# Four broadcasts moved from SyncE's DMA queue, slot 40, to ScalarE's own queue, slot 41

## The reference

```python
h = tok(x)                      # 4x4 patches: 256 tokens of 64 per image, 16 pixels attended per token
h = h + mamba(layernorm(h))     # two selective scans (forward, backward), 128 channels, 16 states
h = h + pkm(layernorm(h))       # 8 heads: product keys pick 16 of 4096 table rows; causal attention; output product
```

```python
x_dbl = x @ W_xproj.T
Bm, Cm = x_dbl[..., 16:32], x_dbl[..., 32:48]       # per token, the same for all channels
h_t = exp(delta_t * A) * h_(t-1) + (delta_t * x_t) * Bm_t
y_t = sum over states of h_t * Cm_t
```

## Time and profile before

| | |
|---|---|
| device time, median of 3 (lowest to highest) | 12621.17 us (12620.08 to 12621.36) |
| profiled execution, its own time | 12642.72 us |
| span of its trace, instructions | 12640.9 us, 260041 |
| mean granted clock of TensorE | 0.973 |
| busy share: PE, PEld, DVE, ACT, POOL | 92%, 72%, 79%, 62%, 74% |
| DMA: packets' share of 16 engines, hardware and software queue | 38.5% and 17.5% |

### The profile page before, as it was taken

How to read it: one execution, slowest core, us unless ns; L and a number is a source line. 1 busy time by engine, 2 the same in 40 slices (tenths; PEclk the granted TensorE clock), 3 DMA queues, 4 the chain that set the end, 5 groups by cost and what they waited for, 6 DMA issues and landing times.

```text
span 12640.9 us, 260041 instructions
## 1 busy us (share of the span) xinstructions
PE 11654.2 (92%) x70396; PEld 9057.1 (72%) x70396; DVE 9999.4 (79%) x38339; ACT 7863.3 (62%) x17926; POOL 9340.6 (74%) x8196
## 2 busy tenths in 40 slices
PE   3999999999999999999999999999999999999999
PEld 2777777777777777777777777777777777777777
DVE  6778878778787787787887877887878778778773
ACT  2666666666666666666666666666666666666665
POOL 1777777777777777777777777777777777777776
PEclk6999999999999999999999999999999999999999
DMA  2555555555555565555555555655555555555554
GB/s 68 155 160 166 154 159 165 150 165 161 154 165 155 157 167 152 161 162 153 165 159 155 165 155 158 168 151 163 161 153 166 156 159 166 149 161 165 152 158 136
DMA packets 1651806, 1975.32 MB, mean 156 GB/s; under 512 B 336239, under 2 KB 1125871, under 8 KB 1649903
## 3 DMA queue, kind: packets, MB, share of 16 engines
q1 hardware_dynamic: 1387950, 1418.48, 38.5%
q0 software_dynamic: 262144, 537.40, 17.5%
HBM read 1881.20 MB, written 73.40 MB: 155 GB/s over the span
## 4 chain that ended last, share of the span: by engine, by line
PE 74%; ACT 11%; DMA 6%; issue 5%; DVE 2%; SPq 2%; POOL 0%; ACTq 0%; DVEq 0%; POOLq 0%
PE bank L1001 20%; PE bank L1037 12%; PE bank L1024 7%; PE bank L1011 6%; ACT bank L1248 4%; DMA moving<-keyspace 4%; PE bank L884 4%; PE bank L931 3%; PE bank L988 3%; PE bank L1061 2%; ACT decay L1189 2%; PE bank L965 2%; PE bank L1055 2%; PE bank L1053 2%; ACT weight L1255 2%
## 5 line engine op out<-in xcount | busy, mean ns | idle before, releaser
L812 POOL DMA_INDIRECT gath<-in_table_dram,rowsT x8192 | 9340.4, 1140 | 3272.0 <-issue 2356.4
L1255 ACT ACTIVATE weight<-bank 128x512 f32<-128x512 f32 x4096 | 2443.2, 596 | 3489.1 <-PE bank L1011 3476.5
L1001 PE MATMUL bank<-weight,rowtab 128*128 128x256 f32 x16384 | 4305.6, 385 | 0.0
L1001 PEld LDWEIGHTS bank<-weight,rowtab 128*128 128x128 f32 x16384 | 3150.3, 193 | 774.2 <-issue 30.6
L1248 ACT ACTIVATE bank<-bank,seventeen 128x512 f32<-128x512 f32 x4096 | 2714.6, 663 | 15.0 <-PE bank L1011 11.9
L1037 PEld LDWEIGHTS bank<-spread,gath 128*128 128x128 f32 x16384 | 2208.6, 196 | 148.6 <-issue 13.9
L1037 PE MATMUL bank<-spread,gath 128*128 128x96 f32 x16384 | 2156.9, 276 | 1.3 <-DMA gath<-in_table_dram,rowsT 0.7
L1024 PE MATMUL bank<-moving,pick_b 96*128 96x512 bf16 x4096 | 1589.4, 388 | 483.3 <-ACT bank L1248 401.5
L1011 PE MATMUL bank<-moving,pick_b 96*128 96x512 bf16 x4096 | 1575.8, 385 | 253.6 <-DMA moving<-keyspace 253.5
L1560 DVE TENSOR_TENSOR_SCAN decay<-decay,wide 128x1024 f32<-128x1024 f32 x512 | 1169.1, 2287 | 150.8 <-issue 78.5
L1812 DVE SCALAR_TENSOR_TENSOR acc<-bank,rrow,acc 128x64 f32<-128x64 f32 x1024 | 243.2, 279 | 1150.0 <-PE bank L1011 1076.3
(11 more groups left out here) (257 smaller groups left out, 16871.1 us busy)
## 6 DMA issues: line engine op xcount, KB each, us to landing
rowtab<-in_tableD_dram SPq DMA_DIRECT2D x2048, 256.0 KB
wide<-states SPq DMA_DIRECT2D x512, 512.0 KB
moving<-keyspace SPq DMA_DIRECT2D x4096, 64.0 KB
gath<-in_table_dram,rowsT POOLq DMA_INDIRECT x8192
moving<-keyspace SPq DMA_DIRECT2D x4096, 32.0 KB
pix<-in_x_dram SPq DMA_DIRECT2D x504, 256.0 KB
keyspace<-split SPq DMA_DIRECT2D x256, 256.0 KB
out_dram<-acc SPq DMA_DIRECT2D x64, 64.0 KB
```

The costliest lines, as they stand in the source:

```text
L812: pool.indirect_dma_start(out=gath[:, u % RING, j, :], out_offset=None, in_=table, in_offset=bass.IndirectOffsetOnAxis(ap=rowsT[k][:, col: ...
L1001: mm(dense_ps[:, 0:TOK], rowtab[:, r, s % 2 * 2 + half, :], weight[s % 2][:, half * TOK:(half + 1) * TOK], start=(s % 16 == 0 and half == ...
L1255: ins = af(weight[s % 2][:], zd_ps[s % 2][:], ACT.Exp, scale=-1.0)
```

## The change

The entry `F.bq` is new in slot 41 of ScalarE's order, behind `F.dc0`. The wait for the store and the four broadcasts are taken out of SyncE's `bc` and stand in that entry, on ScalarE's queue. SyncE's `bc` keeps the waits ahead of the store and the store itself, so that `m43` comes right behind the store.

```diff
-41 w40+0 a2.5+0 l41+0 F.dc0+2
+41 w40+0 a2.5+0 l41+0 F.dc0+2 F.bq+2
...
                 sp.wait_ge(xd_copied, a + 1)
                 sp.dma_start(states.rearrange("y q (n l) -> (y q n) l", l=TOK), xd[:]).then_inc(xd_stored, 16)
-                sp.wait_ge(xd_stored, a * 16 + 16)
-                for q in range(4):
-                    sp.dma_start(quarter[q], states[0, q:q + 1, :].to_broadcast([P, 4 * TOK])).then_inc(bc_loaded[q], 16)
...
+                if name == "bq":
+                    act.wait_ge(xd_stored, a * 16 + 16)
+                    for q in range(4):
+                        act.dma_start(quarter[q], states[0, q:q + 1, :].to_broadcast([P, 4 * TOK])).then_inc(bc_loaded[q], 16)
```

## The result

The changed kernel took 12559.39 us (median of 5 runs, 12538.33 to 12570.78), the kernel before 12620.08 us beside it (5 runs, 12614.22 to 12621.36). The ratio is 0.9946 [0.9935, 0.9958]: 61 us faster, in place of the forecast 130. The profiled execution took 12570.78 us, its span 12569.0, against 12642.72 and 12640.9 before. In its profile the overs stand at L1008 (before L1011), the exponents at L1021, the gather matmuls at L1034, the gathers at L809, the limits at L1249, and the four broadcasts at L1184, now on ScalarE.

A forecast was written before the change was run, and what follows sets the result against it. PE bounds the kernel, stalling on keys once per image. Of 6.1 - 1.1 = 5.0 us, gathers let it keep 2.6; less 0.5 for lower clock, 2.1 times 62 is 130 us: 12490 us predicted, range 12330 to 12600.

The forecast's parts named there:

- What is taken away, 6.1 us per image: PE, slots 42 to 44: 4.1 us of waiting for keys plus 2.0 us of lower clock, removed per image.
- The step that failed: SyncE's queue: keys go out 3.0 us earlier with no 2 MB before them, so PE's key wait nearly vanishes.
- the wait for `moving` at under 30 us: Sign in the profile after: PE's wait for keys falls from 253.5 to under 30 us.
- the second rival: Slot 45's keys late behind the block: 3 us wait, 1.2 us lower clock, total 12571 us; chance 0.08.
- ScalarE's issues, 1.1 us per image: ScalarE between `dc0` and `w41`: four issues take 1.91 us, delay `z42`, and PE waits 1.1 us.
- The third rival: ScalarE's issues between `dc0` and `w41` become the stall, up to 12764 us; chance 0.09 slower, 0.09 within 0.2%.
- VectorE's `B0` later but hidden: VectorE: `B0` comes 0 to 4 us later, hidden by its 4.78 us wait for PE at `negmax`.
- The gathers bound what PE keeps: Gathers, parts g3.1 to g3.6: PE keeps 2.6 of its 5.0 us, before 0.5 us of lower clock.
- the forecast 2.4: PE near slot 61: 2.4 us per image come back as a wait for gathers.
- the lower clock behind it: PE after the wait for gathers near slot 61: 0.5 us per image lost to a lower clock.
- The prediction's row of a wait in one piece: PE before slot 43's overs: 5.19 us of waiting for keys had 2.0 us of lower clock behind it.
- in place of 130: Sign in the profile after: GpSimd's wait for PE falls by about 130 us.

The follow-up runs named there:

- e5: Changed kernel with one broadcast quarter each in slots 41, 43, 45 and 47 on ScalarE, ring of 8 gathered parts for 4; 12280.38 us, 0.9709.
- e11: Changed kernel with broadcasts of 64 columns in place of 1024 and a ring of 8 gathered parts in place of 4; 12263.22 us, 0.9702.
- e10: Kernel before with all four broadcasts on SyncE's queue behind the keys of slot 44, ring of 8 gathered parts for 4; 12469.18 us, 0.9861.
- e6: Changed kernel with a ring of 8 gathered parts in place of 4; 12538.21 us, 0.9911 of the kernel before.
- e2: Changed kernel with one broadcast quarter each in slots 41, 43, 45 and 47, on ScalarE's queue, ring still 4; 12557.72 us, 0.9939.
- e1: Changed kernel with the four broadcasts bringing 64 columns each in place of 1024, same issues and descriptors; 12590.31 us, 0.9960.
- e8: Changed kernel with each partition of a broadcast reading its own 4 KB table row in place of one shared row; 12526.17 us, 0.9905.

## Why the prediction was half right

**What is taken away, 6.1 us per image: right.** Slots 42 to 44 of the kernel before lie 6.1 us above those of e5, and e11 gains 378 us, or 6.1 times 62.

**The step that failed** is in the first part of the change: with the broadcasts gone from SyncE's queue, "2 MB no longer stand before them in their queue", and from it the wait for `moving` at under 30 us, so that a wait for slot 45's keys stood in the sum at nothing. True for slots 43 and 44, whose keys now go out before the block. Slot 45's keys go out 0.4 us behind the last broadcast, and though they stand in another queue they land with the block: medians of 15.7 and 15.95 us after the store's issue, 9.7 us after their own issue, where a load of keys with no block before it takes about 2.5 to 3.5. Of 253.5 us of waiting, 137.7 are left. This was the second rival, given 0.08, with 9 us and more of landing, 3 us of wait and a total of 12571; the landing in the image shown is 9.00, the wait 137.7 / 62 = 2.2 us per image, the total 12559. It had named slot 45's keys. Its price was near too: 3 us of wait and 1.2 of lower clock forecast, 2.31 + 1.43 measured. The argument that decided against it, that the keys are in another queue, was worth little here, and no row of the kernel before had shown two such queues at once. The Trainium skill, DMA: Bandwidth & Descriptors, has both sides. Issuing engines are not separate DMA queues says that another issuer saves only issue time; e10 against e6 agrees, as far as it goes. Queues, rings and completion order says that an engine takes turns between queues packet by packet; the trace shows such turns, but late. In the image shown, the keys' queue (q1) and the block's (q10), first from the keys' issue at 6962.10 to 6966.00, then to 6969.50 (packets, MB, share of 16 engines):

```profile
q10 hardware_dynamic: 243, 0.90, 75.5%
...
q1 hardware_dynamic: 2, 0.00, 0.4%
```

```profile
q10 hardware_dynamic: 237, 0.84, 70.1%
...
q1 hardware_dynamic: 197, 0.09, 9.7%
```

For 3.9 us next to none of the keys' packets run; then they run nearly one for one with the block's, but they are of 512 bytes and the block's of 4 KB. Over the images the first packet of slot 45's keys runs 4.7 us after their issue (median), that of slot 43's keys, which have no block before them, 1.37 us after. So the second queue did not let the keys pass.

**ScalarE's issues, 1.1 us per image: over-sized.** Slot 42 takes 0.32 us more than in e2 and e5. The working set the four issues behind the four activations; they run beside them, and the block goes out 2.7 us later than before (4.18 us after the store's issue against 1.48, medians), not 4.0. In 35 of the 56 images no issue takes over 0.56 us and slot 42 takes 2.56 us, as in e2 and e5: nothing is lost. In the other 21 one issue takes 0.95 to 2.28 us, as the 1.51 us in the image shown, and slot 42 takes 3.42 us on the mean. In e6, the same four issues with the longer ring, slot 42 takes 2.58 us. By line, whole span (ns min, median, max), the issues are

```profile
L1184 ACTq DMA_DIRECT2D wide<-states x256: 326/454/2277, 100.2 to 12150.0; - x128
```

with a median of 454 ns against SyncE's 433 of the earlier trace rows. The Trainium skill, Perfetto Trace Analysis, section DMA Instruction — HWDGE (DVE, Sync), says that a sequencer's wait for the lock of the descriptor generator is inside the reported duration. The 18 issues on ScalarE over 1.2 us agree with it: all ran while SyncE issued too, and none of the 184 issues that SyncE did not overlap took over 0.80. But 54 that it did overlap were not long, and SyncE's issue of 1.93 us at 6962.72 is no evidence, as the kernel before, with no issue on ScalarE, has issues of keys up to 1.79 us. Why some are long, and fewer so with the longer ring, is not shown. The third rival, that the issues become the stall, did not happen.

**VectorE's `B0` later but hidden: right.** It waits for the broadcast 67.2 us in 60 waits, longest 5.1, and slots 46 and 47 of PE take 1.91 and 2.49 us before and after. That the cover is the wait for PE at `negmax` is not shown: this wait falls from 342.2 us to 172.9, but with the longer ring it is 154.2 in e6, where `B0` waits 61.1 us, and 150.9 in e11, where `B0` hardly waits (2.9).

**The gathers bound what PE keeps: right in kind, shown by e2 and e5, under-sized.** In e2, where PE truly is freed, it keeps (12640.72 - 12557.72) / 62 = 1.3 us per image of the 6.1; the forecast had 2.1. The wait is 184.7 / 62 = 3.0 us, near the forecast 2.4, though in slots 55 to 59 more than near slot 61. The term that was mis-sized is the lower clock behind it, put at 0.5 us. It is 6.1 - 3.0 - 1.3 = 1.8, as ScalarE's issues cost nothing there (slot 42 takes 2.56 us in e2 and in e5). The cores' mean granted clocks say the same, e2 first, e5 second:

```profile
core 0: 12556.6 us, clock 0.979
```

```profile
core 0: 12259.8 us, clock 0.987
```

With two levels, a clock of 0.979 is 4.2% of the span at the lower one, or 527 us, and 0.987 is 2.6%, or 319 us. The difference is 3.4 us per image, and work at half the clock loses half of it, 1.7 us. The prediction's row of a wait in one piece, 2.0 us behind 5.19, would have given 0.9 for 2.4 us; it took 0.5, because 1.03 us of idle in pieces left the clock alone. In the e2 image above, 3.86 us in one piece had 6.7 us at 0.53 behind it.

In the changed kernel itself, slot 45's keys held PE back again, so the gathers seldom became the bound (30.9 us), GpSimd's wait for PE fell by 40 us in place of 130, and the total came out inside the range by luck, for a reason that had 0.08. Slots 43 and 44 did run at a nearly full clock (0.98 and 0.96 on the mean): four table matmuls take 1.03 us at 6967.61 where the earlier trace rows had 1.91. Slot 45, for which the forecast had nothing, took the lower clock in their place.

**Left open.** Why the first packets of keys wait 4.7 us behind a block on another queue is not shown; only that the delay goes with the bytes in flight (e1, e11), in part with the rows read (e8), and little with the queue (e6, e10). e1 and e11 make each packet of the block smaller as well as the whole. A block on ScalarE's queue that goes out as early as e10's was not run, and no third queue was tried for the keys.

## What to carry to other kernels

A large transfer delayed the small load issued behind it, on its own queue and on another: ask which small load follows it within its landing time and who waits for that, and cut the block into pieces that land between the loads, before looking for another queue. When a stall of one engine is removed, find the buffer that limits the next producer's lead: five changes to the transfer's place, queue or size gained 0.4 to 0.6% with a ring of four (other rows, in e8, 0.95%) and the ring alone gained nothing, while spreading and ring together gained 2.9%. Price a new wait with the clock that follows it, by a row in which a wait of that size came in one piece.

## What the hardware showed that was not expected

Issues of transfers on ScalarE ran beside its own activations: four issues, 1.78 us together at the median, delayed slot 42 by nothing in 35 of 56 images, and only a long one (0.95 to 2.28 us) delayed it. Long issues on ScalarE, 18 over 1.2 us, came only while SyncE issued too. And a load of 96 KB, issued 0.4 us behind 2 MB of another queue, landed with the end of that block, 9.7 us later, at an engine share of 0.97: its first packet ran 4.7 us after the issue, and from then on its packets of 512 bytes took turns with the block's of 4 KB.
